# The last layer's opening with dt made ahead of C's pieces, two products of du moved to VectorE, and a shorter postponed tail in the third layer

## The chip, the cores and the metric

The kernel runs on one core of a Trainium2 chip. The metric is the device time of one execution in microseconds (us); the time named for a kernel is the median of several executions. Inside the profile, times count from the start of the profiled execution's span.

## What is computed

A graph network of four layers over 2048 nodes with 128 features and one 2048 x 2048 adjacency matrix; each layer is a residual followed by a layer norm. Only the last two matter here:

```python
# third layer (L2): attention, mask from adj
x = h @ weight; el = x @ a_l; er = x @ a_r
attn = where(adj != 0, exp(leaky_relu(el[:, None] + er[None, :], 0.2)), 0)
out = (attn / max(attn.sum(-1), 1e-12)) @ x + b
# last layer (L3): graph convolution, layer norm, and a Mamba block
h = layernorm(relu(adj @ x @ gcn_w + gcn_b)) * ln_g + ln_b
xc, z = split(h @ w_in); u = silu(conv4(xc) + conv_b)
dbc = u @ w_xp
dt = softplus(dbc[:, :8] @ w_dt + b_dt); B = dbc[:, 8:24]; C = dbc[:, 24:]
dA = exp(dt[:, :, None] * -exp(A_log)); dBu = dt[:, :, None] * B[:, None, :] * u[:, :, None]
hst = dAt * hst + dBut; ys = hst @ Ct          # a scan over the 2048 nodes, 16 states, 256 channels
y = (ys + u * D_skip) * silu(z); out = y @ w_out
```

## The kernel before

Everything is one program with hand-written queues: for each engine (PE is TensorE, ACT is ScalarE, DVE is VectorE, POOL is GpSimd, SP starts the DMAs) a function `later_*` issues its instructions in a fixed order, and semaphores join them. An engine does its instructions strictly in the order written, so a wait holds up all that is written behind it on that engine.

**Third layer.** The sum over the 16 row tiles `jt` runs on PE (`weighted`, L969): for each `jt`, 16 output tiles `it` with two matmuls each. The left factors `q2[jt % 4]` (2048 columns, four buffers) are made by DVE for even `jt`, by ACT (L599, L601) for odd `jt`, and masked by DVE (L1350); making tile `jt` waits until PE has finished `jt - 4` (`q2_used`). The first `NT - LAST` row tiles run tile by tile over all outputs; the last `LAST` (3) are postponed and run output by output, after a wait for all of `q2`, so that the outputs are finished in turn (`l2_mm`) and DVE can normalize them quarter by quarter (`after_layer2`, L1362 to L1369; `norm`). The output sums lie in six PSUM banks, three output tiles each; the first quarter needs banks 0 and 1, that is six output tiles. As each quarter of X is scaled (ACT L512, DVE L1207 for the last one), PE starts the adjacency product of the last layer (`a_part`, L992) with it.

**Last layer.** The nodes are cut into 4 chunks of 512 columns. For a chunk: `a_part` (16 row tiles, two matmuls of 512 columns each), `a_copy` (ACT), `gcn` (PE, L1000 and L1002), `relu` (ACT L615), mean and variance on DVE (`h_spread`, L1389), the root on ACT (`h_norm`), `h_rescale` (DVE L1398), transposes (`h_fill`), `ht_copy` (ACT L628), the convolution as matmuls (`conv_part`, L1018), `u_out` (ACT L640), `dbc_product` (L1032), `dbc_copy` (ACT). Then dt in blocks: `dt_product` (PE L1045), `dt_abs` (ACT L709), `dt_log` (ACT, an exp L715 and a log L717), `softplus` (DVE L1420). In chunk 0 dt has four blocks of half channels, `q` = 0 to 3; in the others two. B and C go to DRAM and come back spread over the partitions: `b_rows` to the tiles `bb`, and `c_rows` to `cc` for the steps that POOL weighs (both L370). For the steps that DVE weighs, C is split into three bf16 pieces: `piece` (an ACT copy of bank 4), `take_off` (PE L1038 subtracts the piece from bank 4), and `spread` (L1067) multiplies the pieces to all partitions.

A chunk has 16 steps, 64 in all (step `k`, `n = k % 16`). Step `k` takes two `decay` (ACT L734, `j = 2k` and `2k + 1`, into three PSUM banks), `make_dbu` on POOL (L470, three buffers), two scans on DVE (L1437), a `weigh` (on POOL L482 where `k % 8` is 0, 1 or 4; else on DVE L1448), and `add_up` on PE (L1089). The products `du = dt * u` of chunk 0 are four POOL instructions (`first_du`, L454); the later chunks' are `make_du`.

The order of chunk 0's opening is written out by hand. ACT (L757 to L768): for `q` = 0, 1, 2 dt's abs, exp and log, then piece `q` of C, then a decay; then block 3, `decay(2)`, `a_copy(1, 1)`, `relu(1, 1)`. PE (L1110 to L1118): four `dt_product`, row tiles 8 and 9 of chunk 1's adjacency product, `take_off(0, 0)`, row tiles 10 and 11, `take_off(0, 1)`, row tiles 12 to 15, `gcn(1, 1)`. POOL (L485 to L489): two products of du, `make_dbu(0)`, two more products, `make_dbu(1)`, `make_dbu(2)`. DVE: four `softplus`, then `scan(0)`, then the loop over the steps, where `scan(k + 1)` is issued ahead of step `k`'s weighing; step 0 also issues `h_spread(1, 1)` and step 1 `h_rescale(1, 1)`. SP: the loads of B's first rows, a wait for chunk 1's adjacency product (`a_mm` at 2; the tiles `cc` lie where the adjacency columns of chunk 1 lay), then C's rows for steps 0 and 1, B's next rows, C's row for step 4.

Of the kernel before, what the change touches and what calls it, by code (L numbers as in the profile page):

```python
# [22 lines left out]
DI = 2  # L23
# [28 lines left out]
def gnn_program(nc, t, out):  # L52
    ctx = ExitStack()
    with ctx:  # L54
# [144 lines left out]
        conv_mm, u_ready, zp_mm, zg_ready = sem("conv_mm"), sem("u_ready"), sem("zp_mm"), sem("zg_ready")  # L199
        dbc_mm, dbc_ev, piece_ev, sub_mm = sem("dbc_mm"), sem("dbc_ev"), sem("piece_ev"), sem("sub_mm")  # L200
        res_mm = sem("res_mm")
        dt2_in, du_first, du2_in = sem("dt2_in"), sem("du_first"), [sem("du2_in%d" % b) for b in range(DI)]
        dt_mm, sp_abs, sp_exp, sp_ln, dt_ready, du_ready = (sem("dt_mm"), sem("sp_abs"), sem("sp_exp"), sem("sp_ln"),
                                                            sem("dt_ready"), sem("du_ready"))
        b_out, b_in = sem("b_out"), [sem("b_in0"), sem("b_in1")]
# [213 lines left out]
        def later_pool(pool):  # L419
            nc.gpsimd.memset(sel[:], 0.0).then_inc(sel_ready, 1)  # L420
            nc.gpsimd.memset(neg[:], 0.0).then_inc(sel_ready, 1)
            for p in range(3):
                pool.wait_ge(sel_ready, p + 2)
                by_state = sel[:].rearrange("p q (s m) -> p (q s) m", s=2)
                nc.gpsimd.affine_select(out=by_state, in_=by_state, compare_op=ALU.not_equal, fill=1.0,
                                        base=-(32 * p + STATES), pattern=[[-1, STATES], [0, HALF]],
                                        channel_multiplier=1).then_inc(sel_ready, 1)
            nc.gpsimd.affine_select(out=neg[:, 32:96], in_=neg[:, 32:96], compare_op=ALU.not_equal, fill=-1.0, base=-32,
                                    pattern=[[-1, 64]], channel_multiplier=1).then_inc(sel_ready, 1)
            pool.wait_ge(l1_mm, 4)  # L430
            nc.gpsimd.memset(x2[:, :, P], 1.0).then_inc(ones_col, 1)  # L431
            pool.wait_ge(w2_in, 32)
            pool.wait_ge(xt_ev, 12)
            nc.gpsimd.tensor_tensor(X, X, b2b.unsqueeze(1).to_broadcast([P, NT, P]), ALU.add).then_inc(x_plus_b, 1)

            pool.wait_ge(w3_in, 16 * 10)
            pool.wait_ge(cw_in, 16)
            taps = cwb.rearrange("p d k -> p k d")
            nc.gpsimd.tensor_tensor(wconv, taps, w_in[:, 0:2, :].rearrange("p b m -> p (b m)").unsqueeze(1)
                                    .to_broadcast([P, TAPS, DI * P]), ALU.mult).then_inc(wconv_ready, 1)  # L440

            def make_du(c, b):

                pool.wait_ge(dt_ready, dt_count(c, b))
                pool.wait_ge(u_ready, 2 * c + b + 1)
                if c >= 2:
                    pool.wait_ge(du2_in[0], 64 * c)
                nc.gpsimd.tensor_tensor(du[:, b, :], dt_[:, b, :], u[:, b, :], ALU.mult).then_inc(du_ready, 1)

            def first_du(q):  # L450

                pool.wait_ge(du2_in[q // 2], 64)
                pool.wait_ge(dt_ready, dt_count(0, q))
                nc.gpsimd.tensor_tensor(du2[0][:, q, :], dt2[0][:, q, :], du2[0][:, q, :], ALU.mult).then_inc(du_first, 1)  # L454

            def make_dbu(k):

                c, n = k // STATES, k % STATES
                group = k // 4
                if k < 2:  # L460
                    pool.wait_ge(du_first, 2 * (k + 1))
                elif n < 2:
                    pool.wait_ge(du2_in[0], 64 * (c + 1))
                if k % 4 == 0:
                    pool.wait_ge(b_in[group % 2], 32 * (group // 2 + 1))
                if k == 2:
                    pool.wait_ge(wconv_ready, 1)
                if k >= 3:
                    pool.wait_ge(scan_done, 2 * (k - 2))
                nc.gpsimd.tensor_tensor(dbu[k % 3], du2[c % 2][:, 2 * (n % 2):2 * (n % 2) + 2, :],  # L470
                                        bb[group % 2][:, pair_of(k) % 2, :].unsqueeze(1).to_broadcast([P, DI, CH]),
                                        ALU.mult).then_inc(dbu_ready, 1)

            def weigh(k):

                p = pool_before(k)
                pool.wait_ge(scan_done, 2 * (k + 1))
                pool.wait_ge(c_in[p % 4], 32 * (p // 4 + 1))
                if p >= 2:
                    earlier = [i for i in range(k) if on_pool(i)][p - 2]  # L480
                    pool.wait_ge(y_mm, sums_with(earlier))
                nc.gpsimd.tensor_tensor(hcp[p % 2], cc[p % 4].unsqueeze(1).to_broadcast([P, DI, CH]), hs[k % 3],  # L482
                                        ALU.mult).then_inc(hcp_ready, 1)

            for k in range(2):  # L485
                for b in range(DI):
                    first_du(2 * k + b)
                make_dbu(k)
            make_dbu(2)  # L489
            for k in range(STEPS):  # L490
                if on_pool(k):
                    weigh(k)
                if k + 3 < STEPS:
                    make_dbu(k + 3)
                if k // STATES + 1 < NCH and k % STATES in (9, 10):
                    make_du(k // STATES + 1, k % STATES - 9)

        def later_act(act):
# [256 lines left out]
                u_out(0, b, 4 + b)  # L755
            exp_and_log()
            dbc_copy(0, 4)  # L757
            for q in range(3):
                dt_abs(0, q, FIRST_DT[q])
                dt_log(0, q)  # L760
                piece(0, q, 4)
                if q:
                    decay(q - 1)
            dt_abs(0, 3, FIRST_DT[3])
            dt_log(0, 3)
            decay(2)
            a_copy(1, 1)
            relu(1, 1)  # L768

            def next_chunk(c, n):  # L770

# [25 lines left out]
            for k in range(STEPS):  # L797
                c, n = k // STATES, k % STATES
                for j in (2 * k + 3, 2 * k + 4):
                    if j < 2 * STEPS:  # L800
                        decay(j)
                if c < NCH - 1:
                    save_state(k)
                if c and n == 1:
# [18 lines left out]
        def later_pe(pe):  # L823
# [145 lines left out]
                return nc.tensor.matmul(sums(it, slice(0, P + 1)), q2[jt % 4][:, it * P:(it + 1) * P], x2[:, jt, :],  # L969
                                        start=(jt == 0 and it % 3 == 0), stop=(jt == NT - 1), skip_group_check=True)  # L970

            LAST = 3
            for jt in range(NT - LAST):
                pe.wait_ge(q2_ready, jt + 1)
                pe.wait_ge(l2_xev, jt // 4 + 1)
# [84 lines left out]
            def spread(k):  # L1060

                c, d = k // STATES, dve_before(k)
                if k % STATES == 0:
                    pe.wait_ge(piece_ev, 3 * (c + 1))
                if d:
                    pe.wait_ge(hcd_ready, d)
                nc.tensor.matmul(PS[:, 4, :], sel[:, pair_of(k), :], pieces[c % 2][0:96, :], start=True,  # L1067
                                 stop=True).then_inc(c_mm, 1)
# [40 lines left out]
            for q in range(4):  # L1109
                dt_product(0, q, FIRST_DT[q])  # L1110
            pe.wait_ge(sel_ready, 6)
            a_part(1, 1, 8, 10)
            take_off(0, 0, 4)
            a_part(1, 1, 10, 12)
            take_off(0, 1, 4)
            a_part(1, 1, 12, NT)
            gcn(1, 1)
            pe.wait_ge(xps_ready, 1)  # L1118

            def next_chunk(c, n):  # L1120
# [75 lines left out]
        def later_dve(dve, link):  # L1196
# [266 lines left out]
            h_rescale(0, 2)  # L1463
            for q in range(4):
                softplus(0, q, FIRST_DT[q])
            scan(0)
            for k in range(STEPS):
                c, n = k // STATES, k % STATES
# [652 lines left out]
```

## Time and profile before

| | us |
|---|---|
| median of 3 executions | 914.15 (908.91 to 914.3) |
| the profiled execution's own time | 913.46 |
| its span in the profile | 911.7 |
| PE, DVE, ACT, POOL busy in the span | 811.1, 686.8, 514.8, 233.7 |
| mean granted TensorE clock | 0.943 |

The profiled execution's own time is 1.8 us over its span; the prediction's sums are made within the span. A row of the timeline gives start, duration, engine, line and operation, merged where instructions of one line follow each other (xN); the bracket at its end is the engine's idle time before it and what ended it. A row of the windows gives busy time and count of each engine in a stretch, then the granted clock as a share of full speed, the DMA share and the GB/s.

### The profile page before, as it was taken

Reading aid. Unit: us, or ns where it says so; the run is one execution under the profiler, and the core shown is the slowest. Engines: PE = TensorE matmul, PEld = TensorE weight load, DVE = VectorE, ACT = ScalarE, POOL = GpSimd, SP = SyncE. Lnnn points to the kernel's source line nnn. Section 1 sums busy time; section 2 is a strip of 40 time slices with the busy share of each in tenths; the row PEclk is TensorE's granted clock in tenths of the full one; section 3 lists DMA queues with packets and bytes.
Section 4 is the critical chain, followed back from the end, with each engine's and each line's share of the span. In section 5 each row is a group of like instructions: output and inputs, shape, how many; then the busy total and the mean of one; then the engine's idle time right before and its main releaser. Section 6 shows DMA issues by size and latency. Waiting matters only on the chain. (4 is left out here: it accounts for less than half of the span.)

```text
span 911.7 us, 11859 instructions
## 1 busy us (share of the span) xinstructions
PE 811.1 (89%) x4180; PEld 516.8 (57%) x4180; DVE 686.8 (75%) x988; ACT 514.8 (56%) x818; POOL 233.7 (26%) x135
## 2 busy tenths in 40 slices
PE   6999988999999999999789989989959979887565
PEld 6655537888888888874345559984323222331211
DVE  3986889999999999607942227864088899899997
ACT  2754537777777777634520127523557577676661
POOL 4000000000000000000000020001298889889993
PEclk8999998999999999999989989999879999997876
DMA  8689986220221121039410000000331713526410
GB/s 285 208 315 336 344 290 253 93 93 0 92 92 40 52 92 46 1 133 422 185 28 0 1 1 1 1 1 23 73 104 40 171 46 99 126 53 155 105 47 12
DMA packets 38960, 101.67 MB, mean 112 GB/s; under 512 B 6113, under 2 KB 11114, under 8 KB 32386
## 3 DMA queue, kind: packets, MB, share of 16 engines
q1 hardware_dynamic: 38354, 100.83, 33.6%
q8 instruction: 24, 0.39, 0.2%
q10 hardware_dynamic: 560, 0.27, 0.1%
q14 instruction: 22, 0.18, 0.1%
HBM read 75.60 MB, written 18.14 MB: 103 GB/s over the span
## 5 line engine op out<-in xcount | busy, mean ns | idle before, releaser
L1871 PE MATMUL PS<-big 128*128 128x256 f32 x768 | 194.6, 385 | 3.4 <-ACT big L1701 3.3
L221 PE MATMUL PS<-ident,big 128*128 128x128 f32 x1123 | 158.7, 281 | 29.0 <-DVE big L1398 8.1
L221 PEld LDWEIGHTS PS<-ident,big 128*128 128x128 f32 x1123 | 137.4, 146 | 52.8 <-issue 20.9
L470 POOL TENSOR_TENSOR big<-big 128x1024 f32<-128x1024 f32 x64 | 149.7, 2358 | 10.6 <-DVE big L1437 9.9
L1871 PEld LDWEIGHTS PS<-big 128*128 128x128 f32 x768 | 133.7, 191 | 21.7 <-ACT big L1701 7.1
L1701 ACT ACTIVATE big<-PS 128x512 f32<-128x512 f32 x192 | 105.1, 599 | 58.6 <-PE PS L221 57.7
L431 POOL MEMSET big<- 128x16 f32 x1 | 0.1, 131 | 520.5 <-PE PS L835 520.5
L1437 DVE TENSOR_TENSOR_SCAN big<-PS,stripes,big 128x512 f32<-128x512 f32 x96 | 116.7, 1263 | 5.8 <-ACT PS L734 3.8
L2070 DVE SCALAR_TENSOR_TENSOR big<-big,rz 128x2048 f32<-128x2048 f32 x48 | 112.7, 2350 | 0.9
L2048 DVE CUSTOM_DVE_ANT_0 big<-big 128x2048 f32<-128x2048 bf16 x48 | 109.7, 2289 | 0.1
L734 ACT ACTIVATE PS<-big,stripes 128x512 f32<-128x512 f32 x128 | 86.1, 685 | 33.8 <-DVE big L1437 33.2
L1691 ACT ACTIVATE big<-big,ymin 128x2048 f32<-128x2048 f32 x48 | 96.3, 2006 | 14.7 <-DVE ymin L2048 14.4
L1089 PE MATMUL PS<-big,stripes 128*64 128x512 f32 x256 | 76.3, 690 | 9.8 <-DVE big L1448 5.5
L333 ACT ACTIVATE big<-PS 128x512 f32<-128x512 f32 (+3 forms) x51 | 29.9, 592 | 79.1 <-PE PS L835 17.2
L969 PE MATMUL PS<-big 128*128 128x129 f32 x512 | 59.6, 280 | 4.5 <-DVE big L1350 4.5
L992 PE MATMUL PS<-big 128*128 128x512 f32 x128 | 61.7, 619 | 0.5 <-ACT big L512 0.5
L969 PEld LDWEIGHTS PS<-big 128*128 128x128 f32 x512 | 59.0, 196 | 5.1 <-DVE big L1350 3.7
L835 PE MATMUL PS<-big 128*128 128x512 f32 x128 | 58.7, 608 | 2.2 <-DVE big L1301 1.5
L1794 PE MATMUL PS<-big 128*128 128x512 f32 x128 | 57.8, 597 | 0.0
L1448 DVE TENSOR_TENSOR big<-PS,big 128x1024 f32<-128x1024 f32 x40 | 47.9, 1199 | 3.9 <-PE PS L1067 3.8
L482 POOL TENSOR_TENSOR big<-big 128x1024 f32<-128x1024 f32 x18 | 42.4, 2357 | 9.8 <-DVE big L1437 9.7
L1437 DVE TENSOR_TENSOR_SCAN big<-PS,big 128x512 f32<-128x512 f32 x32 | 37.3, 1205 | 8.9 <-ACT PS L734 5.0
(211 smaller groups left out, 973.9 us busy)
## 6 DMA issues: line engine op xcount, KB each, us to landing
big<-in_adj SPq DMA_DIRECT2D x16, 2048.0 KB, 9.3
big<-at_dram SPq DMA_DIRECT2D x4, 4096.0 KB, 28.0
at_dram<-big SPq DMA_DIRECT2D x3, 4096.0 KB, 17.0
big<-b_dram SPq DMA_DIRECT2D x32, 256.0 KB, 4.3
big<-big SPq DMA_DIRECT2D x24, 256.0 KB, 4.0
big<-b_dram SPq DMA_DIRECT2D x36, 128.0 KB, 4.0
at_dram<-big SPq DMA_DIRECT2D x1, 3072.0 KB, 18.6
big<-e_dram SPq DMA_DIRECT2D x3, 1024.0 KB, 6.3
```

Of the source, the lines that this page charges most:

```text
L221: return nc.tensor.transpose(PS[:, bank, col:col + P], src, ident[:])
L470: nc.gpsimd.tensor_tensor(dbu[k % 3], du2[c % 2][:, 2 * (n % 2):2 * (n % 2) + 2, :], bb[group % 2][:, pair_of(k) % 2, :].unsqueeze(1).to_b ...
L734: nc.scalar.activation(PS[:, 5 + j % 3, :], dt2[c % 2][:, q, :], ACT.Exp, scale=na[:, q, pair_of(k):pair_of(k) + 1]).then_inc(da_ready, 1)
L969: return nc.tensor.matmul(sums(it, slice(0, P + 1)), q2[jt % 4][:, it * P:(it + 1) * P], x2[:, jt, :], start=(jt == 0 and it % 3 == 0), st ...
L992: m = nc.tensor.matmul(PS[:, bank, :], X[:, jt, :], AT[:, jt, c * CH:(c + 1) * CH], start=(jt == 0), stop=(jt == NT - 1))
L1089: m = nc.tensor.matmul(PS[h * HALF:(h + 1) * HALF, 2 + n % 2, :], fold, v[:, h, :], start=False, stop=(n >= STATES - 2), skip_group_check= ...
L1437: nc.vector.tensor_tensor_scan(hs[k % 3][:, b, :], PS[:, 5 + j % 3, :], dbu[k % 3][:, b, :], state[:, pair_of(k), 2 * (n % 2) + b:2 * (n % ...
L1691: e = nc.scalar.activation(w[s], w[s], ACT.Exp, bias=ymin[:, s:s + 1], scale=-1.0, accum_out=zsum[:, s:s + 1])
L1701: nc.scalar.activation(qt[v % 4], PS[:, v % 4, :], ACT.Copy).then_inc(qt_ready, 1)
L1871: m = nc.tensor.matmul(PS[:, 4 + k // 3, 0:256], hw[:, jt, h, :], qt[v % 4][:, 256 * c:256 * c + 256], start=(h == 0 and jt == 0), stop=(h ...
L2048: m = nc.vector.tensor_tensor_reduce(out=w[s], in0=bm[2 * pair + j], in1=eb[0][h], scale=1.0, scalar=3.0e38, op0=ALU.add, op1=ALU.min, acc ...
L2070: m = nc.vector.scalar_tensor_tensor(w[s], w[s], rz[:, s:s + 1], aw[pair][:, j, :], ALU.mult, ALU.mult)
```

## The change

Third layer: `LAST` is 2 in place of 3. Last layer's opening: ACT makes all four blocks of dt with only `decay(0)` among them, then `decay(1)`, `decay(2)`, then piece 0 of C, then `a_copy(1, 1)`; pieces 1 and 2 and `relu(1, 1)` go into the loop behind decays 3, 5 and 4. PE runs row tiles 8 to 15 in one go, then `take_off(0, 0)`, `gcn(1, 1)`, `take_off(0, 1)`. Two of the four products of du (blocks 2 and 3) are made by DVE behind the third and the fourth `softplus`; POOL makes the first two and then `make_dbu` for steps 0, 1, 2. `spread` waits for the third piece where it is the first spread of all.

```diff
--- before.py
+++ after.py
@@ -199,7 +199,7 @@
         conv_mm, u_ready, zp_mm, zg_ready = sem("conv_mm"), sem("u_ready"), sem("zp_mm"), sem("zg_ready")
         dbc_mm, dbc_ev, piece_ev, sub_mm = sem("dbc_mm"), sem("dbc_ev"), sem("piece_ev"), sem("sub_mm")
         res_mm = sem("res_mm")
-        dt2_in, du_first, du2_in = sem("dt2_in"), sem("du_first"), [sem("du2_in%d" % b) for b in range(DI)]
+        dt2_in, du_first, du_second, du2_in = sem("dt2_in"), sem("du_first"), sem("du_second"), [sem("du2_in%d" % b) for b in range(DI)]
         dt_mm, sp_abs, sp_exp, sp_ln, dt_ready, du_ready = (sem("dt_mm"), sem("sp_abs"), sem("sp_exp"), sem("sp_ln"),
                                                             sem("dt_ready"), sem("du_ready"))
         b_out, b_in = sem("b_out"), [sem("b_in0"), sem("b_in1")]
@@ -458,7 +458,7 @@
                 c, n = k // STATES, k % STATES
                 group = k // 4
                 if k < 2:
-                    pool.wait_ge(du_first, 2 * (k + 1))
+                    pool.wait_ge(du_second if k else du_first, 2)
                 elif n < 2:
                     pool.wait_ge(du2_in[0], 64 * (c + 1))
                 if k % 4 == 0:
@@ -482,11 +482,10 @@
                 nc.gpsimd.tensor_tensor(hcp[p % 2], cc[p % 4].unsqueeze(1).to_broadcast([P, DI, CH]), hs[k % 3],
                                         ALU.mult).then_inc(hcp_ready, 1)
 
-            for k in range(2):
-                for b in range(DI):
-                    first_du(2 * k + b)
+            for q in range(DI):
+                first_du(q)
+            for k in range(3):
                 make_dbu(k)
-            make_dbu(2)
             for k in range(STEPS):
                 if on_pool(k):
                     weigh(k)
@@ -755,17 +754,15 @@
                 u_out(0, b, 4 + b)
             exp_and_log()
             dbc_copy(0, 4)
-            for q in range(3):
+            for q in range(4):
                 dt_abs(0, q, FIRST_DT[q])
                 dt_log(0, q)
-                piece(0, q, 4)
-                if q:
-                    decay(q - 1)
-            dt_abs(0, 3, FIRST_DT[3])
-            dt_log(0, 3)
+                if q == 2:
+                    decay(0)
+            decay(1)
             decay(2)
+            piece(0, 0, 4)
             a_copy(1, 1)
-            relu(1, 1)
 
             def next_chunk(c, n):
 
@@ -799,6 +796,12 @@
                 for j in (2 * k + 3, 2 * k + 4):
                     if j < 2 * STEPS:
                         decay(j)
+                    if j == 3:
+                        piece(0, 1, 4)
+                    elif j == 4:
+                        relu(1, 1)
+                    elif j == 5:
+                        piece(0, 2, 4)
                 if c < NCH - 1:
                     save_state(k)
                 if c and n == 1:
@@ -969,7 +972,7 @@
                 return nc.tensor.matmul(sums(it, slice(0, P + 1)), q2[jt % 4][:, it * P:(it + 1) * P], x2[:, jt, :],
                                         start=(jt == 0 and it % 3 == 0), stop=(jt == NT - 1), skip_group_check=True)
 
-            LAST = 3
+            LAST = 2
             for jt in range(NT - LAST):
                 pe.wait_ge(q2_ready, jt + 1)
                 pe.wait_ge(l2_xev, jt // 4 + 1)
@@ -1060,8 +1063,8 @@
             def spread(k):
 
                 c, d = k // STATES, dve_before(k)
-                if k % STATES == 0:
-                    pe.wait_ge(piece_ev, 3 * (c + 1))
+                if not d:
+                    pe.wait_ge(piece_ev, 3)
                 if d:
                     pe.wait_ge(hcd_ready, d)
                 nc.tensor.matmul(PS[:, 4, :], sel[:, pair_of(k), :], pieces[c % 2][0:96, :], start=True,
@@ -1109,12 +1112,10 @@
             for q in range(4):
                 dt_product(0, q, FIRST_DT[q])
             pe.wait_ge(sel_ready, 6)
-            a_part(1, 1, 8, 10)
+            a_part(1, 1, 8, NT)
             take_off(0, 0, 4)
-            a_part(1, 1, 10, 12)
+            gcn(1, 1)
             take_off(0, 1, 4)
-            a_part(1, 1, 12, NT)
-            gcn(1, 1)
             pe.wait_ge(xps_ready, 1)
 
             def next_chunk(c, n):
@@ -1463,6 +1464,10 @@
             h_rescale(0, 2)
             for q in range(4):
                 softplus(0, q, FIRST_DT[q])
+                if q >= 2:
+                    dve.wait_ge(du2_in[1], 64)
+                    dve.wait_ge(dt_ready, dt_count(0, q))
+                    nc.vector.tensor_tensor(du2[0][:, q, :], dt2[0][:, q, :], du2[0][:, q, :], ALU.mult).then_inc(du_second, 1)
             scan(0)
             for k in range(STEPS):
                 c, n = k // STATES, k % STATES
```

## Rows read from the trace of the kernel before

**Rows 1.** The page: busy time, share and instructions of each engine.

```profile
PE 811.1 (89%) x4180; PEld 516.8 (57%) x4180; DVE 686.8 (75%) x988; ACT 514.8 (56%) x818; POOL 233.7 (26%) x135
```

**Rows 2.** Timeline of PE, third layer's sum (start, duration, instruction).

```profile
555.02 43.16 PE L969 MATMUL PS<-big 128*128 128x129 f32 x384 [0.23 <-DVE big L1350]
601.23 12.63 PE L969 MATMUL PS<-big 128*128 128x129 f32 x96 [3.05 <-DVE big L1350]
```

**Rows 3.** Timelines of ACT and DVE at the third layer's end.

```profile
594.65 2.10 ACT L599 ACTIVATE big<-es,deg,bj 128x2048 f32<-128x2048 f32 x1 [3.02 <-PE PS L969]
...
598.88 2.29 DVE L1350 SCALAR_TENSOR_TENSOR big<-big 128x2048 f32<-128x2048 f32 x1 [1.27 <-ACT big L601]
607.26 0.23 DVE L1362 TENSOR_TENSOR zi<-PS,ci 128x3 f32<-128x3 f32 x2 [6.09 <-PE PS L969]
```

**Rows 4.** Windows (PE, PEld, DVE, ACT, POOL busy; clock; DMA), 602.5 to 605.9 us.

```profile
602.50:605.90 3.40, 3.40 (x18) 3.40 (x18) 0.00 (x0) 0.00 (x0) 0.00 (x0) 0.50 0.00 0
```

**Rows 5.** Timeline of the step from the third layer to the last.

```profile
614.35 14.86 PE L992 MATMUL PS<-big 128*128 128x512 f32 x34 [0.50 <-ACT big L512]
```

**Rows 6.** Timeline of ACT in the last layer's opening.

```profile
652.46 0.63 ACT L717 ACTIVATE big<-big 128x512 f32<-128x512 f32 x1
656.62 0.59 ACT L333 ACTIVATE big<-PS 96x512 bf16<-96x512 f32 x1 [3.53 <-PE PS L1038]
...
663.04 0.57 ACT L333 ACTIVATE big<-PS 128x512 f32<-128x512 f32 x1
```

**Rows 7.** Timeline of PE in the last layer's opening.

```profile
652.37 3.78 PE L992 MATMUL PS<-big 128*128 128x512 f32 x4
655.94 0.63 PE L1038 MATMUL PS<-big,neg 96*96 96x512 bf16 x1
656.37 2.24 PE L992 MATMUL PS<-big 128*128 128x512 f32 x4
...
658.88 3.70 PE L992 MATMUL PS<-big 128*128 128x512 f32 x8
663.67 1.12 PE L1000 MATMUL PS<-wt 1*128 1x512 f32 x2 [1.08 <-ACT big L333]
...
674.17 1.11 PE L221 MATMUL PS<-ident,big 128*128 128x128 f32 x4 [8.08 <-DVE big L1398]
```

**Rows 8.** Timeline of DVE and POOL in the last layer's opening.

```profile
655.88 2.35 POOL L470 TENSOR_TENSOR big<-big 128x1024 f32<-128x1024 f32 x1 [0.66 <-DMA big<-b_dram]
...
663.16 2.33 DVE L1437 TENSOR_TENSOR_SCAN big<-PS,big 128x512 f32<-128x512 f32 x2
663.39 1.26 POOL L454 TENSOR_TENSOR big<-big 128x512 f32<-128x512 f32 x1 [1.62 <-DVE big L1420]
...
667.11 2.34 DVE L1437 TENSOR_TENSOR_SCAN big<-PS,big 128x512 f32<-128x512 f32 x2 [1.62 <-POOL big L470]
...
669.32 2.35 POOL L482 TENSOR_TENSOR big<-big 128x1024 f32<-128x1024 f32 x1
...
672.78 1.34 DVE L1398 TENSOR_SCALAR big<-PS,mv,rstd 128x128 f32<-128x128 f32 x4
```

**Rows 9.** Groups by form: DVE's products of two tensors of 128x512 in SBUF.

```profile
L1260 DVE TENSOR_TENSOR big<-big 128x512 f32<-128x512 f32 x8 | 5.5, 682 | 2.4 <-ACT big L536 2.4
```

**Rows 10.** DMA issues, 640 to 680 us (KB each, median us to landing).

```profile
big<-b_dram SPq DMA_DIRECT2D x8, 128.0 KB, 3.2
```

**Rows 11.** Windows by the microsecond where the clock changes.

```profile
650.00:651.00 1.00, 1.00 (x3) 0.49 (x2) 0.17 (x1) 0.97 (x3) 0.00 (x0) 0.63 0.03 4
...
657.00:658.00 1.00, 1.00 (x3) 0.38 (x2) 0.00 (x0) 1.00 (x3) 1.00 (x1) 0.96 0.00 0
...
677.00:678.00 1.00, 1.00 (x2) 0.12 (x1) 0.47 (x1) 0.42 (x2) 1.00 (x1) 0.72 1.07 225
```

**Rows 12.** Timeline behind the opening: where DVE next waits.

```profile
689.80 0.69 ACT L640 ACTIVATE ns<-PS,conv_b 128x512 f32<-128x512 f32 x1 [2.63 <-PE PS L1018]
...
692.53 1.22 DVE L1437 TENSOR_TENSOR_SCAN big<-PS,big 128x512 f32<-128x512 f32 x1 [3.42 <-ACT PS L734]
```

## Prediction

> **What bounds the kernel now.** I read the page first: PE is busy 89% of the span and DVE 75% [rows 1], but these are averages over stages with different limits. So I read the timelines of the two stages that the diff touches, each engine by itself, then the windows for TensorE's clock, then the next wait behind the opening.
>
> The end of the third layer is a relay. PE does 384 matmuls in 43.16 us, 0.112 us each, so a row tile (32 of them) costs 3.6 us. Then it stands for 3.05 us and does the last 96, the postponed three row tiles, in 12.63 us [rows 2]. The 3.05 us are the wait for all of q2: ACT starts the last left factor at 594.65, when PE has given a buffer back, two ACT passes follow, and DVE masks it from 598.88 to 601.17 [rows 3]. That is 6.5 us from buffer to factor, against one row tile of work left for PE (3.6 us). After the gap the granted clock reads 0.50 from 602.5 to 605.9 [rows 4], the 1.2 GHz level: 96 matmuls at 0.112 us would be 10.8 us, so the fall costs 1.84 us. DVE stands until six output tiles are there and starts at 607.26 [rows 3]. From there DVE's chain of quarters sets the pace; PE's next work starts at 614.35, only 0.50 us after PE came free, and its 34 matmuls of 0.437 us fill 14.86 us [rows 5].
>
> In the last layer's opening ACT is the engine that holds the others, and it holds them for PE: after block 1 of dt it stands 3.53 us for the first subtraction from bank 4 [rows 6], which lies behind two row tiles of the adjacency product that run at 0.95 us a matmul in place of 0.44 [rows 7]. The clock is at 0.50 from about 650.3 to 657.1 [rows 11]. So blocks 2 and 3 of dt come late, and the first scan, which DVE issues behind the fourth softplus, starts at 663.16, although its dBu was there at 658.23. The second scan waits 1.62 us more, because POOL must make the fourth product of du first (663.39) and then dBu [rows 8]. Behind it hangs chunk 1: its rescaling on DVE starts at 672.78 [rows 8], PE stands 8.08 us for it and goes on at 674.17 [rows 7], and the next large wait of DVE (3.42 us, through ACT's 2.63 us for PE's convolution, [rows 12]) is the end of that same PE chain.
>
> **Third layer, LAST = 2.** PE keeps one more row tile ahead of the wait. It came to the end of the 13th at 598.18 (where the row of the 384 ends [rows 2]) and now does the 14th, ready long before, until 601.75; q2 is complete at 601.17, so the wait is gone. The postponed part is 64 matmuls; DVE's first quarter needs six output tiles of two row tiles, 24 matmuls or 2.7 us at full clock, so it starts at 604.5 in place of 607.26. DVE's chain behind it is unchanged: everything later moves up by 2.7 us. PE now ends at 608.95, 4.9 us earlier, but that is not gained, since X's first quarter comes at 614.35 - 2.7 = 611.65. So a gap of 2.7 us appears on PE that was 0.50 us. What is late next is this gap: the gap of 3.05 us was followed by a fall that cost 1.84 us, and here the 34 matmuls fill their stretch, so a fall would be paid in full. The bounds are 0 and 1.84 us (3.4 if the low level lasts 6.8 us, as it did in the opening [rows 11]). The gap is a little shorter than the one that was followed by a fall; I take half, 0.9. Gain of this part: 2.7 - 0.9 = 1.8 us.
>
> The Trainium skill ("TensorE: Matmul & The Clock Gate", "What's actually happening") says that the reduced clock is the default and sustained activity lifts it, and that the moment varies from run to run. By that rule alone the new gap would bring the fall, and the part's gain would be 0.9 us. The fall after the 3.05 us agrees with it; no row here shows a gap of 2.7 us.
>
> **Opening, ACT.** Without pieces between them, an abs, an exp and a log follow each other 1.82 us apart (0.61, 0.66, 0.55 from start to start). The log of block 1 starts at 652.0 (before 652.46 [rows 6]); block 2's abs at 652.5, its log ends at 654.4; `decay(0)` takes 0.6; block 3's log ends at 656.9 in place of 662.5. Then `decay(1)`, `decay(2)` and piece 0 until 658.6. `a_copy(1, 1)` stood at 663.04 [rows 6] and now waits for PE. Queued behind it is `decay(3)`, and for that the second half of scan 1.
>
> **Opening, PE.** The 16 matmuls and two subtractions took from 652.37 to 662.58 [rows 7]. The subtractions go, 0.43 and 0.34 us from start to start: the product ends at 661.8. So `a_copy` runs to 662.4, `gcn` needs 2.2 us (663.67 to 665.9 before [rows 7]), its relu ends at 665.3 (before 666.5), and `decay(3)` at 663.0. The spread's new wait costs nothing: piece 2 is there at 666.5 and the first weighing on DVE is later than 672. The pieces and the relu in the loop take the places of ACT's idle time between decays.
>
> **Opening, DVE.** Added are two products of two 128x512 tensors, 0.68 us each [rows 9]. The first lies in the wait for block 3's log (655.2 to 655.9, hidden by 1.7 us of idle time). The second runs from 657.6 to 658.3, while dBu of step 0 ends at 658.23 (its B rows landed at 655.9, unchanged [rows 8]): 0.1 us shows; without this cover it is 0.7. Scan 0 starts at 658.3, 4.8 us earlier. Scan 1's first half follows, its second waits for `decay(3)` and ends at 664.2. The spread of chunk 1 waits for the relu and ends at 666.6, scan 2 at 668.9, and the rescaling starts at 668.9 in place of 672.78: 3.9 us.
>
> **Opening, POOL.** Two products of 1.26 us go; `make_dbu` for steps 1 and 2 run from 658.3 to 663.0. Then a wait takes over that was hidden: step 0's weighing needs C's rows, which SP may load only behind chunk 1's adjacency product. Two loads of 128 KB, issued from 661.8 on with 0.6 us between them, land 3.2 us after their issue [rows 10]: 665.6. So the weighing starts at 665.6 in place of 669.32 [rows 8]: 3.7 us. I take 3.8 for the opening, between the two chains. The bounds: 0 (PE's chain behind the rescaling runs at the low clock until 677.6 [rows 11]; if the level lasts 3.8 us longer for starting earlier, it gives 1.9 back, and C's rows could come late as well) and 8 (below).
>
> **Sum.** 1.8 + 3.8 = 5.6 us: the profiled execution's 913.46 becomes 907.9. It stands 0.7 us under the median of 914.15, so I give 908.
>
> **Rivals.** *The opening's gain is taken back behind it.* DVE waits 3.42 us for the convolution [rows 12]; were that chain held by something that doesn't move with the rescaling (the clock, PE's turn among the sums), only the third layer's part and a rest of the opening would be left: about 2.7 us, 911. For it: PE has hardly an idle us from 674 to 690. Against it: that chain starts at the rescaling.
>
> *The clock does not fall in the denser stages.* No fall behind the third layer (+0.9), none in the opening: the four matmuls at 0.95 us would take 1.8 in place of 3.8, dt's products another us less, and the chain from 674.17 loses 1.7 less. That is 0.9 + 2.6 + 1.7 = 5.2 us more, 903. For it: fewer and shorter gaps before it; against it: the four dt products with 9 rows remain, and the clock fell right behind them.
>
> *Slower: the clock stays at the low level through both denser stretches.* In the product of chunk 0 the level would last 6.8 us (3.4 lost, 2.5 more than counted), and in chunk 1's product the 12 matmuls that now run at full level would cost 0.44 us more each, 5.2, which puts off C's rows, the relu and `decay(3)` together. That is 7.7 us against 5.6 of gain: 2.1 slower, 915.5. It decides from 11 us more at the low level than now, since a us there loses 0.5. Against it: in the trace the level rose again within 6.8 us each time that PE was at work [rows 4, 11].
>
> **How the numbers follow.** The forecast (906 to 910.5) has 0.52, the taken-back case 0.2, the higher clock 0.22, the slower case 0.06. The range reaches from near the high-clock case to the taken-back case with the spread of the median's three values (5.4 us): 903.5 to 912. A measurement of this kernel can tell about 1%, 9 us, from no change; under 905 lies nearly all of the higher clock's case, 0.2; over 923 almost nothing, 0.03; within 1% is 0.77.
>
> **What would show it.** PE's 3.05 us before the postponed part gone, DVE's first quarter 2.7 us earlier, a gap of 2 to 3 us before L992. In the opening, counted from the start of L992: scan 0 about 4.8 us earlier, no wait of ACT before block 2, a wait of ACT for `a_copy`, POOL idle for some 2 us before its first weighing with C's rows as the releaser, the rescaling 3.9 us earlier, and the same again at DVE's wait for the convolution. It is wrong if scan 1 or 2 starts no earlier, if PE's chain from the transposes to the second `u_out` is longer than 15.6 us, or if the clock reads 0.50 in the first product.

## The result, and the profile after

The changed kernel takes 908.35 us (median of 20) where the one before takes 911.86 (median of 20): ratio 0.9963, 95% interval 0.9947 to 0.9979. Measured a second time it is 0.9941 (0.9921 to 0.9961). So it is 3 to 5 us faster; 908 was forecast. One of the twenty executions of the changed kernel took 2016.56 us; it is left out of the ratio and does not move the median. The kernel before had 914.15 as the median of three executions and 911.86 of twenty, which is worth remembering: the gain in the ratio is smaller than 914.15 - 908.35.

The timelines of the changed kernel, third layer's end (DVE, then PE; start, duration, instruction, idle time before):

```profile
603.30 2.29 DVE L1351 SCALAR_TENSOR_TENSOR big<-big 128x2048 f32<-128x2048 f32 x1 [1.27 <-ACT big L600]
608.96 0.23 DVE L1363 TENSOR_TENSOR zi<-PS,ci 128x3 f32<-128x3 f32 x2 [3.37 <-PE PS L972]
...
616.06 16.55 PE L995 MATMUL PS<-big 128*128 128x512 f32 x34 [2.74 <-ACT big L511]
```

This execution reached the third layer's end 4.42 us later than the profiled one of before (603.30 against 598.88 in [rows 3]); 3.2 us of this are there by 21 us, in work that the change doesn't touch (PE's first matmul starts at 7.51 against 6.43, behind a load, a group of 32 small matmuls takes 6.99 us against 4.90, and the transposes behind it start at 21.02 against 17.81). So absolute times don't compare, and distances do. From the last masking to DVE's first quarter it is 5.66 us against 8.38 [rows 3]: 2.72 us gained, as forecast (2.7). The gap ahead of PE's first product is there (2.74, forecast 2.7), and the 34 matmuls take 16.55 us in place of 14.86 [rows 5]: 1.69 us given back. The windows of one microsecond say why (the third number from the right is the clock):

```profile
617.00:618.00 1.00, 1.00 (x3) 0.47 (x2) 0.97 (x6) 0.43 (x2) 0.00 (x0) 0.75 0.00 0
```

It reads 0.50 in the next two microseconds and 1.00 again from 621 on: a fall to the 1.2 GHz level, as behind the gap of 3.05 us in the kernel before [rows 4].

The last layer's opening in the same profile (rows of DVE, POOL, ACT and PE, with others between them left out):

```profile
658.64 0.69 DVE L1470 TENSOR_TENSOR big<-big 128x512 f32<-128x512 f32 x1
659.55 2.36 POOL L470 TENSOR_TENSOR big<-big 128x1024 f32<-128x1024 f32 x1 [1.40 <-DMA big<-b_dram]
661.07 1.39 DVE L1470 TENSOR_TENSOR big<-big 128x512 f32<-128x512 f32 x1
662.37 2.32 DVE L1438 TENSOR_TENSOR_SCAN big<-PS,big 128x512 f32<-128x512 f32 x2
662.53 4.65 POOL L470 TENSOR_TENSOR big<-big 128x1024 f32<-128x1024 f32 x2 [0.63 <-DVE big L1470]
663.62 0.60 ACT L333 ACTIVATE big<-PS 128x512 f32<-128x512 f32 x1 [1.68 <-PE PS L995]
664.91 2.34 DVE L1438 TENSOR_TENSOR_SCAN big<-PS,big 128x512 f32<-128x512 f32 x2 [0.21 <-POOL big L470]
667.14 2.34 POOL L482 TENSOR_TENSOR big<-big 128x1024 f32<-128x1024 f32 x1
670.58 1.34 DVE L1399 TENSOR_SCALAR big<-PS,mv,rstd 128x128 f32<-128x128 f32 x4
671.98 1.11 PE L221 MATMUL PS<-ident,big 128*128 128x128 f32 x4 [3.16 <-DVE big L1399]
...
690.41 1.22 DVE L1438 TENSOR_TENSOR_SCAN big<-PS,big 128x512 f32<-128x512 f32 x1 [3.48 <-ACT PS L733]
```

These answer to [rows 6 to 8] and [rows 12]. Counted from the first copy of the last layer (631.80 here, 628.39 before), scan 0 starts 4.2 us earlier, chunk 1's rescaling 5.6 us earlier, and DVE's wait for the convolution ends 5.5 us earlier. PE's wait of 8.08 us is 3.16 us. `a_copy` waits for PE (1.68 us), as forecast. Two things differ: POOL's first weighing (667.14) did not wait for C's rows, and DVE's second product took 1.39 us in place of 0.69. From 690.41 to the end of the span are 219.2 us, as before (219.2): between these two profiles, what the opening gives is kept.

### The profile page after: what moved, and what is told of

Its sections match the earlier page's. It is cut to its first block and busy times, and to the rows that moved or that the text cites. A ratio compares the mean times of both kernels' runs of the same rounds, so it can differ in the third digit from the quotient of the medians.

```text
span 909.6 us, 11861 instructions
## 1 busy us (share of the span) xinstructions
PE 813.6 (89%) x4180; PEld 519.0 (57%) x4180; DVE 689.1 (76%) x990; ACT 514.3 (57%) x818; POOL 231.2 (25%) x133
## 5 line engine op out<-in xcount | busy, mean ns | idle before, releaser
L1876 PEld LDWEIGHTS PS<-big 128*128 128x128 f32 x768 | 134.1, 191 | 21.6 <-ACT big L1706 6.9
L972 PE MATMUL PS<-big 128*128 128x129 f32 x512 | 57.7, 275 | 1.4 <-DVE big L1351 1.4
L972 PEld LDWEIGHTS PS<-big 128*128 128x128 f32 x512 | 57.3, 192 | 1.9 <-issue 1.7
L995 PEld LDWEIGHTS PS<-big 128*128 128x128 f32 x128 | 24.5, 199 | 35.1 <-issue 31.9
```

The source lines that it names most:

```text
L995: m = nc.tensor.matmul(PS[:, bank, :], X[:, jt, :], AT[:, jt, c * CH:(c + 1) * CH], start=(jt == 0), stop=(jt == NT - 1))
L1876: m = nc.tensor.matmul(PS[:, 4 + k // 3, 0:256], hw[:, jt, h, :], qt[v % 4][:, 256 * c:256 * c + 256], start=(h == 0 and jt == 0), stop=(h ...
```

## The experiments

To compare executions that differ by some us in their first 600, I cut the way into four distances between marks on DVE and ACT: from the last masking of q2 to DVE's first quarter (third layer), on to the first copy of the last layer (its first product), on to chunk 1's rescaling (the opening), and on to the scan behind DVE's wait for the convolution. "Low" is how long the clock was at its low level (0.50), added up from windows of 1 us: within the third distance and, behind the comma, in the next low stretch. That second stretch begins 1.5 to 7 us before the end of the third distance, while PE mostly waits for the rescaling, and reaches into the fourth.

```
kernel                 3rd layer  product  opening  convolution   sum     low
before                      8.38    21.13    44.39        19.75   93.65   6.8, 10.2
last2_only                  5.65    22.84    43.03        20.89   92.41   3.4, 13.6
last2_gap_filled            5.66    21.13    41.37        20.85   89.01   0,   13.6
opening_only                6.74    21.14    38.77        20.26   86.91   3.4,  6.8
changed                     5.66    22.84    38.78        19.83   87.11   3.4,  6.8
changed_again               5.66    21.14    40.42        20.02   87.24   6.8,  6.8
gap_filled                  5.67    21.13    40.43        19.94   87.17   6.8,  6.8
du_all_pool                 5.66    22.83    40.27        20.55   89.31   3.4, 10.2
later_du_dve                5.66    22.83    38.77        19.78   87.04   3.4,  6.8
interleaved                 5.66    22.83    43.15        20.81   92.45  10.2, 10.2
both_filled                 5.66    21.13    40.43        18.09   85.31   6.8,  0
clock_kept                  5.66    21.13    39.04        18.10   83.93   0,    0
clock_kept_again            5.66    21.13    39.62        18.10   84.51   0,    0
```

Two parts of the span lie outside these distances. The last masking starts anywhere from 597.1 to 603.3 us. And from the last mark to the end of the span it is 219.2 us in three profiles (before, changed, clock_kept), in which the low level fills 53 us of it, and 219.7 to 222.0 us in the other ten, with 60 to 69 us at the low level; the two executions of the changed kernel alone differ by 2.3 us there (219.2 and 221.5). So the sums show what the edits do in their stages, and the device times carry the scatter of the rest as well.

**The third layer's edit alone.** In the kernel before:

```diff
-            LAST = 3
+            LAST = 2
```

> The kernel before with the third layer's edit alone (two postponed row tiles). Theory A (my account): DVE's first quarter 2.7 us earlier, PE then stands 2.7 us ahead of the last layer's first product, and a fall of the clock costs 1.7 us of it where it comes: 0.9 to 1.8 us faster than before, ratio 0.998 to 0.999. Rival B (the measured 3.5 us are short of 5.6 because the fall comes in every execution and takes nearly all): 0 to 1 us. Rival C (the opening is what falls short): 2.7 us faster, ratio 0.997.

Measured: 0.9993 (0.9966 to 1.002), 0.6 us, no difference that can be told; the interval reaches from nothing to the 2.7 us of rival C. The trace has both halves, 2.73 us gained ahead of DVE's first quarter and 1.71 us lost in the product:

```profile
612.53 16.55 PE L992 MATMUL PS<-big 128*128 128x512 f32 x34 [2.75 <-ACT big L512]
```

By its middle value the time fits rival B, the trace fits theory A with a fall; the times can't part them. The next run shows what neither had counted: the old gap of 3.05 us does not always bring the fall.

**The opening's edits alone.** In the changed kernel:

```diff
-            LAST = 2
+            LAST = 3
```

> The changed kernel with three postponed row tiles again, so the opening's edits alone. Theory A: 3.8 us faster, up to 5.5 where the low clock of the opening is shorter, ratio 0.994 to 0.996. Rival B: 2.5 to 3.5 us, nearly the whole measured gain. Rival C (the opening's gain is taken back behind it): under 1.5 us.

Measured: 0.9972 (0.9944 to 0.9999), 2.6 us. The middle value lies in rival B's range, but the interval (0.1 to 5.1 us) leaves room for all three; the trace's opening is 5.6 us shorter than before, at a low level of 3.4 us in place of 6.8. In its third layer PE stands 3.05 us as in the kernel before, yet the 96 matmuls behind it take 10.99 us where they took 12.63 [rows 2]; the clock reads 1.00 throughout:

```profile
599.47 10.99 PE L972 MATMUL PS<-big 128*128 128x129 f32 x96 [3.05 <-DVE big L1351]
```

So the kernel before pays 1.64 us for its gap in one execution and nothing in another. The edit is worth 2.7 us against the first and 1.1 us against the second, less 1.7 us where the new gap brings a fall.

**The new gap filled.** In the changed kernel, ahead of the wait for X's first quarter:

```diff
             for q in range(4):
+                if q == 0:
+                    for i in range(3):
+                        nc.tensor.matmul(PS[:, 7, :], ident[:], es[:, 0:CH], start=True, stop=True)
                 pe.wait_ge(x_ready, 8 + q + 1)
```

> The changed kernel with three matmuls of 128x512 (six on PE, 2.6 us, into a PSUM bank that nothing reads) issued between the third layer's sum and the last layer's first product, to keep PE busy in the new gap of 2.7 us; no computed value changes. Theory A (idle time of PE brings the fall): the clock reads 1.00 through the 34 matmuls, they take 14.9 us and not 16.5, and the kernel is 1 to 1.7 us faster than the changed one. Rival (the fall has another cause, as the kind of work or a fixed time): the same 16.5 us and the same time as the changed kernel, or slower by what the six matmuls push back.

Measured: 0.9945 (0.9922 to 0.9968). The product takes its 14.86 us:

```profile
612.07 14.86 PE L995 MATMUL PS<-big 128*128 128x512 f32 x34 [0.16 <-ACT big L511]
```

That the idle time brings the fall stands in the traces: with the gap open the fall came in five profiled executions of six, with it filled in none of five. That filling it makes the kernel faster does not. The medians are 908.03 and 908.35, and the sum of the distances is 87.17 us against 87.11: the 1.7 us won in the product are gone in the opening, where the low level lasted 6.8 us in place of 3.4 (40.43 against 38.78 us).

**The same in the kernel before.** Two postponed row tiles and the three matmuls, without the opening.

> The kernel before with two postponed row tiles and the three filling matmuls, without any edit of the opening. Theory A (the third layer's 2.7 us were there and the fall in the new gap took them back): 1.1 to 2.7 us faster than before, ratio 0.997 to 0.999, where the edit without filling gave 0.9993; the 34 matmuls take 14.9 us. Rival (what the third layer gives is lost ahead of the opening whatever the clock): ratio 0.9993 again, and the first copy of the last layer comes no earlier.

Measured: 0.9973 (0.9948 to 0.9998), 2.5 us; its gap before the product is 0.16 us and the 34 matmuls take 14.86 us. With the clock held, the third layer's edit gives about what it promised, though the interval (0.2 to 4.7 us) also holds the 0.6 us of the edit without filling.

**All four products of du on POOL.** In the changed kernel, POOL's old order (two products, dBu 0, two products, dBu 1 and 2) and no product on DVE (the first of its three pieces):

```diff
-                    pool.wait_ge(du_second if k else du_first, 2)
+                    pool.wait_ge(du_first, 2 * (k + 1))
```

> The changed kernel with all four products of du on POOL again, in the old order; the other edits stay. Theory A: POOL makes product 3 of du from about 661.0 (span of the changed kernel) or behind step 0's dBu at 661.9, two products of 1.27 us between dBu 0 and dBu 1, so the second scan starts some 2 us later and POOL's first weighing with it, but chunk 1's rescaling only by what scan 1 and 2 are late: 1 to 2 us slower than the changed kernel. Rival (DVE's second product, 1.39 us beside POOL in place of 0.69, takes back what it gave, and C's rows set the pace anyway): within 0.5 us of the changed kernel.

Measured: 0.9958 (0.9934 to 0.9982), not to be told from the changed kernel. In the trace the second scan starts 34.6 us behind the first copy, where it was 33.1 in the changed kernel, and the opening is 1.5 us longer than in the executions with as long a low level. The second scan on DVE shows the wait:

```profile
661.67 2.34 DVE L1439 TENSOR_TENSOR_SCAN big<-PS,big 128x512 f32<-128x512 f32 x2 [2.53 <-POOL big L470]
```

The rest of the chain hangs on it: chunk 1's spread starts 2.25 us behind the second scan's start here as in the changed kernel (663.92 - 661.67, 667.16 - 664.91). Theory A holds in the stage; the times are too coarse to confirm 1.5 us.

**The products of the later chunks on DVE too.**

```diff
+                    nc.vector.tensor_tensor(du[:, b, :], dt_[:, b, :], u[:, b, :], ALU.mult).then_inc(du_ready, 1)
```

behind `softplus(c + 1, n - 8)`, with its waits, and `make_du` gone from POOL.

> The changed kernel with the six products of du of chunks 1 to 3 on DVE too, behind the softplus of their block, where POOL is at work all the time. It measures what a DVE product of two SBUF tensors costs beside POOL. Theory A (DVE stands until POOL's instruction is through, as 1.39 and 1.05 us in place of 0.69 suggest): the six take between 0.7 and 3 us each, mean well over 1 us. Rival (the 1.39 us were a chance of that place): 0.69 us each. For the time: DVE gains 4 to 10 us of work, POOL loses 7.6; at best the same time as the changed kernel, at worst 6 us slower.

Measured: 0.9984 (0.9967 to 1.0002), which by the middle values is 2 or 4 us less gain than the changed kernel's (0.9963 and 0.9941); the interval overlaps that of the first. The six products, by their source line (shortest, median and longest in ns):

```profile
L1499 DVE TENSOR_TENSOR big<-big,ns x6: 1203/1395/2212, 698.7 to 828.5; 128x512 f32<-128x512 f32 x6
```

Their mean is 1.58 us; the same form with POOL idle took 0.68 [rows 9]. The rival falls.

**PE's idle stretches in the opening filled as well.** gap_filled, and around the first spread:

```diff
+            nc.tensor.matmul(PS[:, 0, :], ident[:], es[:, 0:CH], start=True, stop=True)
             spread(next(k for k in range(STEPS) if spreads(k)))
+            for i in range(3):
+                nc.tensor.matmul(PS[:, 0, :], ident[:], es[:, 0:CH], start=True, stop=True)
```

> The changed kernel with its two idle stretches of PE filled: the three matmuls ahead of the first product as in gap_filled, and four more of the same kind (eight on PE, into a bank that nothing reads before it is written anew) around the first spread, where PE stood 1.62 and 3.16 us. Theory A: the clock stays at 1.00 from the gcn of chunk 1 to the convolution; the four skip products take 1.8 us in place of 3.2 to 3.6, and DVE's wait of 3.5 to 4.1 us for the convolution shrinks by 1.5 to 2 us: 1.5 us faster than gap_filled, 2.5 to 3 us faster than the changed kernel. Rival (the chain behind the rescaling is not what DVE waits for in the end): DVE's later waits grow by the same, no gain over gap_filled.

Measured: 0.9945 (0.9923 to 0.9967). The clock reads 1.00 from 654 us on, when chunk 1's product is more than half done; the four matmuls behind the transposes (L1082, the products with D_skip) take 1.88 us where they took 3.12 to 3.62, and DVE's wait for the convolution is less than half:

```profile
666.77 1.88 PE L1082 MATMUL PS<-ns,wt 128*128 128x512 f32 x4
...
682.97 1.22 DVE L1444 TENSOR_TENSOR_SCAN big<-PS,big 128x512 f32<-128x512 f32 x1 [1.69 <-ACT PS L733]
```

The last distance is 18.1 us in all three profiles with this filling and 19.75 to 20.9 in the other ten, and the sum is 1.9 us less than gap_filled's. The time does not show it: the ratio is gap_filled's own (0.9945), which is what the rival said, with intervals some 4 us wide.

**The dt products between row tiles.** In the changed kernel:

```diff
-            a_part(1, 1, 7, 8)
             for q in range(4):
+                a_part(1, 1, 7 + q, 8 + q)
                 dt_product(0, q, FIRST_DT[q])
             pe.wait_ge(sel_ready, 6)
-            a_part(1, 1, 8, NT)
+            a_part(1, 1, 11, NT)
```

> The changed kernel with the four dt products each behind one row tile of chunk 1's product, in place of four in a row; the same matmuls in another order. Theory A (the low clock in the opening comes from the matmuls with 9 rows and PE's short waits around them): the low level there becomes shorter or goes, chunk 1's product ends 1 to 2 us earlier, and with it relu and rescaling; DVE's waits fall by as much: 0.5 to 2 us faster than the changed kernel. Rival (the kind of matmul does not matter): the low level stays 3.4 or 6.8 us long, and each block of dt comes up to 0.9 us later, so 0 to 1 us slower.

Measured: 0.9968 (0.994 to 0.9996). A miss: the low level lasted 10.2 us in the opening here, longer than in any other run, and the opening is 43.15 us. The order of the matmuls alone does not keep the clock up. Here the first of DVE's two products fell beside POOL's dBu 0 and took 1.88 us.

**Both together, twice.** both_filled and the order of interleaved.

> both_filled and interleaved together. Theory A: the clock reads 1.00 from the third layer to the convolution of chunk 1, and the gains add: 3 to 5 us faster than the changed kernel, ratio to the kernel before 0.990 to 0.993. Rival: one of the low stretches stays and with it its 1.7 us; ratio 0.994 or more.

> The version with the clock kept up once more, beside the changed kernel on one chip. Theory A: 2 to 3.5 us faster than the changed kernel, ratio to before 0.990 to 0.994. Rival (chance of the earlier execution): within 1 us of the changed kernel.

Measured: 0.994 (0.9915 to 0.9964) and 0.9916 (0.9885 to 0.9947), medians 906.72 and 906.65. In the windows of 20 us the clock stays at 1.00 from the third layer's end to the convolution, in both profiled executions (clock_kept's are shown):

```profile
600.00:620.00 20.00, 19.84 (x97) 12.79 (x97) 14.24 (x80) 6.62 (x20) 0.00 (x0) 1.00 0.03 12
620.00:640.00 20.00, 19.90 (x55) 8.67 (x53) 3.12 (x13) 4.43 (x7) 2.87 (x1) 1.00 0.12 30
640.00:660.00 20.00, 18.55 (x45) 6.65 (x44) 9.05 (x11) 16.04 (x27) 10.11 (x6) 1.00 0.39 100
660.00:680.00 20.00, 18.18 (x55) 6.30 (x55) 18.32 (x27) 11.41 (x22) 20.00 (x9) 1.00 0.34 88
```

By the medians it is some 1.5 us ahead of the changed kernel, less than the 3 to 5 and the 2 to 3.5 us expected, and no faster than both_filled (906.07); the first ratio, 0.994, is the number that I had given to its rival, the second lies in theory A's range, and the intervals overlap. The sums of the distances, 3.2 and 2.6 us under the changed kernel's, say where it falls short: with the clock up all the way the opening takes 39.04 and 39.62 us, more than the 38.78 of the changed kernel with 3.4 us of low level. The relu of chunk 1 is done early there (659.11 and 661.24), and its spread starts only behind the second scan (659.97 and 662.46), which waits for dBu 1 and so for DVE's products beside POOL. In clock_kept_again the first product took 2.63 us:

```profile
653.71 2.63 DVE L1476 TENSOR_TENSOR big<-big 128x512 f32<-128x512 f32 x1
```

**The changed kernel again.**

> The changed kernel itself, on the same chip as the next two. Its first measurement gave 0.9963 of the kernel before. Theory A (third layer 0.2 to 1 us, opening 3.8 to 5.5): 0.9945 to 0.9965. Rival (the stages' gain is partly lost elsewhere in the program): 0.997 or more.

Measured: 0.9941 (0.9921 to 0.9961). This is the one execution with the new gap open and no fall:

```profile
612.51 14.86 PE L995 MATMUL PS<-big 128*128 128x512 f32 x34 [2.73 <-ACT big L511]
```

Its low level in the opening was 6.8 us long, not 3.4, so that the sum of its distances is within 0.2 us of the first execution's.

## Why the prediction was right, and where it was off

**The time, 908 against 908.35,** is better than the prediction was. I started from one execution of 913.46 us and a median of three of 914.15, where twenty give 911.86, and I forecast a gain of 5.6 us, where 3.5 were measured against those twenty. The two errors, of some 2 us each, cancel. Even the last step was loose: 0.7 us over 907.9 would have been 908.6.

**Third layer, gain of 2.7 us:** right (5.66 against 8.38, 2.72), but only against an execution in which the old gap had brought a fall. I took that fall as given because the one trace that I had showed it; opening_only shows that the same gap can pass without. Against that case the edit gives 1.1 us (5.66 against 6.74).

**Third layer, the new gap:** its length was right (2.73 to 2.75 us). I took 0.9 us for the fall, half of the 1.84 of before. It is 1.70 us in five executions of six, 1.4 on average. This is the mis-sized term, together with the one above: 1.8 us were forecast for this part. Taking the old gap's fall in one execution of two (all that was seen) the traces give, as an estimate from eight profiles, 1.9 - 1.4 = 0.5 us, and the run of the edit alone gave 0.6. The rule that I set beside the row (the Trainium skill, "TensorE: Matmul & The Clock Gate", "What's actually happening": the reduced clock is the default, activity lifts it, the moment varies from run to run) was nearer than my half. The traces agree with it as far as six of the eight open gaps brought the fall; that a gap must bring it was my own addition, and two did not.

**Opening, 3.8 us:** right. Executions are to be compared at equal length of the low level ahead of the rescaling. With 6.8 us of it the opening takes 44.39 us in the old order and 40.42 and 40.43 in the new; with 3.4 us, 43.03 and 38.77 to 38.78. That is 4.0 and 4.25 us, where I had 3.9 for the rescaling. The 5.6 us between the two profiles hold 1.6 us that belong to the clock and not to the change. (One profile fits neither group: last2_gap_filled has the old order, no low level before 660 us, and 41.37 us.) The long wait of ACT for PE is gone, and the rescaling, not the first scan, carries the gain on: scan 0 came 4.2 us earlier (4.8 forecast), and the wait for the convolution ended 5.5 us earlier. Of the opening's edits only the products of du were tested by themselves (1.5 us in du_all_pool's trace); what ACT's and PE's new orders give apart is read from the timelines and not shown by a run.

**POOL's new wait for C's rows:** right in the executions in which chunk 1's product is late (gap_filled, changed_again, both_filled: 1.8 to 2.0 us; interleaved: 1.2; opening_only and later_du_dve: 0.3 and 0.6), absent in the profiled changed kernel, where the low level was short:

```profile
663.13 2.35 POOL L482 TENSOR_TENSOR big<-big 128x1024 f32<-128x1024 f32 x1 [1.99 <-DMA big<-b_dram]
```

(gap_filled's POOL timeline.) It costs nothing that shows in the opening: in gap_filled and in changed_again the spread of chunk 1 waits 1.07 us for the relu, and not for POOL.

**DVE's second product, 0.1 us:** wrong. It took 1.39 us beside POOL and ended 0.55 us behind dBu 0, so scan 0 and dBu 1 started about that much late. I had scan 1 wait for `decay(3)`, behind chunk 1's product; that holds where the low level lasted 6.8 us (gap_filled and changed_again: 0.70 us), but in the changed kernel's first profile scan 1 waited for dBu 1 (664.91) and `decay(3)` was there at 664.80. The sum still hardly feels it there, because scan 1 and chunk 1's relu, which the spread needs as well, end together (667.25 and 667.10). With the clock up (clock_kept) it is the path that counts.

**Rivals.** The taken-back case did not happen at the convolution: DVE's wait for it ended 5.5 us earlier, and the rest took 219.2 us in both profiles. That the rest is always the same is not shown (221.5 us in changed_again). The case of the higher clock happened in neither profile of the changed kernel; clock_kept shows what it is worth, 87.1 to 87.2 us against 83.9 to 84.5, about 3 us where I had 5.2. The slower case did not come; the longest low stretch in the opening (interleaved) would nearly have done it, with a sum of 92.45 against 93.65.

The total: 5.6 forecast; 0.5 + 4.1 = 4.6 by the traces; 3.4 and 5.4 by the two measurements, with intervals of 1.9 to 4.8 and 3.6 to 7.2. The forecast lies outside the first and inside the second.

## What to carry to other kernels

Removing a wait of TensorE by letting it run ahead moves its idle time to the next dependence; look where the gap goes and what stands behind it, since a gap of under 3 us was followed here by a fall that cost 1.7 us of a dense stretch in five profiled executions of six. Where a single profile shows a fall of the clock, treat it as one draw: compare stages only at equal length of the low level. A few matmuls into a bank that nothing reads held the clock across such gaps here without delaying the work behind them; whether the whole gains by it has to be measured, since the low level came back longer in the next stage.

## What the runs showed of the hardware that I had not expected

A product of two SBUF tensors on DVE (0.69 us alone) does not run beside one of POOL's here; started while one is under way, it ends 0.55 to 0.56 us behind the end of POOL's. In the changed kernel POOL's dBu ends at 661.91 and the product at 662.46; in opening_only 654.76 and 655.32:

```profile
652.37 2.39 POOL L470 TENSOR_TENSOR big<-big 128x1024 f32<-128x1024 f32 x1 [1.03 <-DMA big<-b_dram]
654.27 1.05 DVE L1470 TENSOR_TENSOR big<-big 128x512 f32<-128x512 f32 x1
```

The scans and the weighings, with one operand in PSUM, keep their durations beside POOL (2.32 to 2.34 us for two scans, 1.2 us for a weighing). The Trainium skill ("GPSIMD Engine Reference", "8. Key points") names contention with DVE instructions of two SBUF inputs; the runs agree and add the size: a product takes 1.58 us on the mean in later_du_dve in place of 0.68. Where the product starts first, POOL's instruction is the longer one: in clock_kept (below) the product kept its 0.69 us, and a dBu that started 0.02 us behind it took 2.89 us in place of 2.36.

```profile
651.79 0.69 DVE L1476 TENSOR_TENSOR big<-big 128x512 f32<-128x512 f32 x1
651.81 2.89 POOL L470 TENSOR_TENSOR big<-big 128x1024 f32<-128x1024 f32 x1 [0.81 <-DMA big<-b_dram]
```

The clock fell in the opening while PE was at work, 5 to 8 us after its last pause (0.87 us), during the dt products with 9 rows or up to 1.1 us behind them (in the kernel before at 650.4, while they ran, and in all profiled executions but three). That the few rows are the cause stays open. Putting row tiles between them did not help alone, and did together with the filling ahead of the first product, in two executions only. And the third execution without the fall (last2_gap_filled) has the four products in a row: with that filling and the four products in a row the fall came in two profiles of three.
